# Other shares of 262 steps per batch among the stages of an audio tower kernel

## The reference, cut to what matters

```python
scores, idx = jax.lax.top_k(sim, 16)                       # 8 heads, two halves of a key, 64 keys each
score = scores[0][..., :, None] + scores[1][..., None, :]
final_scores, pk_idx = jax.lax.top_k(score, 16)            # 16 of the 256 sums
final_scores = softmax(final_scores)
k = einsum('bnhk,bnhkd->bnhd', final_scores, keys_table[ind])      # ind: 4096 rows per head
v = einsum('bnhk,bnhkd->bnhd', final_scores, values_table[ind])
attn = softmax(where(causal, q @ k, lowest));  out = attn @ v;  return out @ Wo
```

## Time and profile before

| what | value |
|---|---|
| three runs, median (lowest to highest) | 7954.98 us (7948.87 to 8025.97) |
| the profiled execution, its own time | 7943.69 us |
| its span, first to last instruction | 7941.9 us |
| mean granted TensorE clock | 0.941 of full |
| PE busy | 6697.2 us, 84% |
| ACT busy | 5005.2 us, 63% |
| POOL busy | 4498.3 us, 57% |
| DVE busy | 4120.9 us, 52% |

### The profile page before, as it was taken

The page is one execution under the profiler, slowest core; times in us unless marked ns, Lnnn a source line. Parts: engine busy times, 40 slices in busy tenths (PEclk is TensorE's granted clock), DMA queues, the critical chain, the costliest instruction groups (busy, mean ns, idle before and its releaser), DMA issues.

```text
span 7941.9 us, 139719 instructions
## 1 busy us (share of the span) xinstructions
PE 6697.2 (84%) x28800; PEld 3500.4 (44%) x28800; DVE 4120.9 (52%) x13711; ACT 5005.2 (63%) x10845; POOL 4498.3 (57%) x4108
## 2 busy tenths in 40 slices
PE   2789798897979889798888979889797988979977
PEld 1445354443535444353443535444353544435533
DVE  7472645627374472646537264562737447273146
ACT  0666576665757666576665657667575766667842
POOL 0575665656565565656556565565656556566610
PEclk9999899998999999899998989999898999999977
DMA  0111111111111111111111111111111111111100
GB/s 29 46 42 34 37 40 38 40 36 36 40 36 39 37 40 36 36 40 38 38 38 38 36 38 41 36 40 36 35 40 36 40 35 40 36 38 44 48 19 13
DMA packets 93887, 294.93 MB, mean 37 GB/s; under 512 B 17879, under 2 KB 26546, under 8 KB 92780
## 3 DMA queue, kind: packets, MB, share of 16 engines
q1 hardware_dynamic: 92748, 285.25, 11.2%
q10 hardware_dynamic: 288, 0.07, 0.0%
HBM read 280.68 MB, written 4.61 MB: 36 GB/s over the span
## 4 chain that ended last, share of the span: by engine, by line
PE 62%; DVE 27%; issue 6%; ACT 4%; DVEq 0%; ACTq 0%; POOL 0%; DMA 0%; SPq 0%; POOLq 0%
PE accu L505 24%; PE dense L491 7%; PE dense L512 7%; DVE picks L1231 6%; PE dense L493 6%; DVE picks L1225 4%; PE sims L623 2%; PE work L629 2%; PE sims L593 2%; DVE store L1235 2%; PE work L668 1%; DVE i L1173 1%; PE work L616 1%; PE work L551 1%; DVE picks L1205 1%
## 5 line engine op out<-in xcount | busy, mean ns | idle before, releaser
L440 POOL TENSOR_TENSOR dense_w<-dense_w,store 128x375 f32<-128x375 f32 x4096 | 4495.9, 1107 | 3092.4 <-ACT dense_w L878 3070.1
L505 PE MATMUL accu<-dense_w,store 128*128 128x375 f32 x8192 | 3365.4, 494 | 186.8 <-POOL dense_w L440 104.5
L883 ACT ACTIVATE past<-dense,edge 128x375 bf16<-128x375 f32 x4096 | 2351.8, 574 | 1195.5 <-PE dense L512 1172.5
L878 ACT ACTIVATE dense_w<-dense 128x375 f32<-128x375 f32 x4096 | 1955.5, 477 | 114.8 <-PE dense L493 107.0
L505 PEld LDWEIGHTS accu<-dense_w,store 128*128 128x128 f32 x8192 | 1430.1, 194 | 554.7 <-issue 334.9
L512 PE MATMUL dense<-store,hot 128*128 128x375 bf16 x4096 | 1338.0, 327 | 163.5 <-ACT past L883 159.4
L491 PE MATMUL dense<-store,spread 96*128 96x375 bf16 x4096 | 1353.1, 330 | 53.0 <-ACT dense_w L878 45.7
L493 PE MATMUL dense<-past,far 128*128 128x375 bf16 x4096 | 1356.8, 331 | 0.0
L512 PEld LDWEIGHTS dense<-store,hot 128*128 128x128 bf16 x4096 | 400.5, 98 | 1490.1 <-issue 1241.3
L491 PEld LDWEIGHTS dense<-store,spread 96*128 96x128 bf16 x4096 | 401.6, 98 | 839.4 <-issue 541.1
L1231 DVE TENSOR_TENSOR picks<-picks 125x2048 uint16<-125x2048 uint16 (+2 forms) x576 | 726.5, 1261 | 76.5
(11 more groups left out here) (248 smaller groups left out, 6497.6 us busy)
## 6 DMA issues: line engine op xcount, KB each, us to landing
store<-in SPq DMA_DIRECT2D x513, 512.0 KB, 3.5
x_in<-in SPq DMA_DIRECT2D x16, 187.5 KB, 2.4
store<-in SPq DMA_DIRECT2D x1, 2048.0 KB, 8.7
queries_kept<-n3T SPq DMA_DIRECT2D x16, 93.8 KB, 3.7
h_saved<-h SPq DMA_DIRECT2D x16, 93.8 KB
store<-queries_kept SPq DMA_DIRECT2D x16, 93.8 KB, 2.3
store<-h_saved SPq DMA_DIRECT2D x16, 93.8 KB
out<-store SPq DMA_DIRECT2D x16, 93.8 KB
```

Of the source, the lines that this page charges most:

```text
L440: nc.gpsimd.tensor_tensor(dense_w[:, i % RING, :], dense_w[:, i % RING, :], first_of[:, i // CHUNKS, :], ALU.mult).then_inc(s["weighed"], 1)
L505: last = mm(accu[:, 0, 0:S], table[:, n % PIECE_RING, i % PIECE, :], dense_w[:, i % RING, :], start=(c == 0), stop=(c == CHUNKS - 1))
L878: fn(dense_w[:, i % RING, :], dense[:, n % 2, 0:S], ACT.Relu).then_inc(s["taken"], 1)
L883: fn(past[:, j % 2, :], coded, ACT.Relu, bias=edge[:, 0:1]).then_inc(s["past"], 1)
```

## The change

Only the constants that share out the slots are changed. The sum stays 262 for each batch.

```diff
-FILL_PREPARE = (4, 3, 3, 4, 5, 4, 4, 4, 5)
-FILL_GRADIENT = (3, 6, 5, 6, 6, 6, 5)
+FILL_PREPARE = (2, 2, 2, 3, 4, 4, 4, 4, 4)
+FILL_GRADIENT = (2, 4, 4, 4, 4, 4, 4)
 PICKS_GRADIENT = (1, 1, 1, 1, 1, 1, 1)
-FILL_FIRST = (8, 18)
-FILL_SECOND = (24, 19)
+FILL_FIRST = (8, 36)
+FILL_SECOND = (34, 32)
 FILL_VO, FILL_QUERY, FIRST_HEAD = (2, 2, 2), 2, 4
-STEPS_A = (6, 6, 6, 6, 6, 6, 8, 8)
-STEPS_B = (6, 6, 6, 6, 6, 6, 6, 6)
+STEPS_A = (5, 5, 5, 5, 5, 5, 6, 5)
+STEPS_B = (5, 5, 5, 5, 5, 5, 4, 4)
 NEXT_FROM = 6
-FILL_LAST = (3, 5)
+FILL_LAST = (2, 4)
```

## The result

The changed kernel takes 7619.83 us, median of three runs (7617.11 to 7624.59), against 7954.98 before: a ratio of 0.9554, 95% interval 0.9471 to 0.9636. The forecast was 7630.

What follows compares the result with a forecast made beforehand. PE is busiest (84%), but DVE's picking ends both rounds, with PE waiting 27.6 us per batch. Removed 44.2 less added 21.7 us is 22.5 per batch, 325 us together: 7955 to 7630 us, range 7540 to 7790.

Steps and rivals of the forecast that it cites:

- The price of a step: Outside the rounds, each removed step gives back 1.18 us; 40 steps per batch are worth 47.2 us.
- Gradient: Of three steps (3.5 us) removed just ahead of L706, 2.4 us are lost; the stage's other steps count fully.
- Heads: Heads 0 to 5: PE moves up by 14.2 us, less 0.6 us for tight places; bounds 7.1 and 14.2.
- First round: Of 17 added steps 10 are free; 7 cost 8.3 us, less 2.9 us at the upper clock: 5.4 us.
- Second round: Of 23 added steps 8 fit the idle time; 15 cost 17.7 us, less 3.9 us at the upper clock: 13.8 us.
- POOL's 1.4 us: Added cost per batch in the rounds: POOL is held up a little longer beside DVE, 1.4 us.
- The 1.1 us for a copy of `accu`: Added cost per batch: one `accu` copy that PE waits out inside its long wait comes out of it.
- DVE binds the attention: Rival in the heads: DVE's picks of tile 2 leave PE only 7.1 us; 16 us per batch, 7725 us; chance 0.2.
- the slower rival: EARLY, preparation, heads: removed steps give back nothing, rounds still cost 21.7 us per batch; 8260 us; chance 0.04.
- POOL's pace for all steps: Rival in the rounds: POOL's 1.7 us holds for all added steps, 11.5 us gained per batch; 7788 us; chance 0.1.
- The full return: Rival in the rounds: all of PE's wait and slow stretches come back, 36.2 us per batch; 7436 us; chance 0.05.
- the fourth rival: Same as the slower rival: removed steps were cover, 8260 us, chance 0.04; sign: PE less busy in EARLY or heads.

Runs made afterwards that it cites:

- each round alone: Two kernels against the one before: only the first round gets more slots (26 to 44), 7798.65 us; only the second (43 to 66), 7748.87 us.
- the second round alone: Kernel before with more slots in the second round only (43 to 66), taken out of EARLY and the heads: 7748.87 us, ratio 0.9743.

## Why the prediction was right

- **What bounds the rounds.** L1261 ended them; with 18 and 23 steps more it doesn't, and the time goes. Shown by the waits (31 to 2) and by each round alone.
- **The price of a step, 1.18 us**, holds in EARLY and preparation to within 1.5 us per stage. It is a price at the upper clock, and the stages' clocks moved: EARLY from 0.97 to 1.00, the preparation from 0.99 to 0.94. The prediction has no term for the clock outside the rounds.
- **Gradient.** "I count 2.4 us, as much as that wait, as lost": the total was 0.9 us off (-9.7 for -10.6). The two slots taken at that place were the weak part of the change: with them back the gradient is 3.4 us shorter, most of it the clock. That I had not seen. Why the clock is lower there isn't settled by the length of the wait, as the two runs with one round alone show.
- **Heads.** 14.2 less 0.6 us expected, 16.9 measured, more than the upper bound. DVE's waits for the scores, 6.34, 3.34 and 4.11 us in the earlier trace rows, are now 0.36, 1.89 and 3.90 us, 7.6 us less where 7.1 were expected, and the end of picking is in time: L475 waits for L1261 nowhere in the loop. Of the further 3 us about 2 can be read from the stage's rows: the granted clock goes from 0.99 to 1.00 of 120 us (1.2 us, an estimate) and PE's idle time from 6.8 to 6.0 us. The last 1 us isn't settled.
- **First round.** +7.4 for +7.7 us, though "10 of the 17 are free" was low: with 37 slots in the round DVE was still last by 2.2 us. DVE ended 4.2 us later in the round than before (56.3 us after its start, not 52.1), and PE had 6.0 us more to do, not 8. So the sum came out nearer than its steps.
- **Second round.** 3.0 us too cheap: +18.2 for +15.2. The term that failed is "the similarities, the products L603 behind them (2.33 us, half of it saved) and a step come at the upper clock, 3.9 us". Only the similarities got faster, and nothing came of it, because L603 starts when PE's branch is through (5.72 us after the similarities began, against 3.97 before), and behind that idle time PE is at the lower clock again. PE had 10.5 us more to do than DVE there, not 18.
- **The small terms.** POOL's 1.4 us: PE's wait for it went from 7.8 to 9.0 us. The 1.1 us for a copy of `accu` that comes out of the long wait didn't show: those waits went from 4.6 us in five to 4.1 in four.
- **The sum.** 22.5 us per batch forecast, 23.8 measured; 325 and 335 us in all. The misses of the second round and of the heads have opposite signs and nearly cancel. The total is closer than its parts, and that is luck.
- **The rivals.** That DVE binds the attention is refuted by the second round alone and by the heads' 103.1 us. Cover that was lost (the slower rival) is seen in one place only, ahead of L706. POOL's pace for all steps is refuted by +7.4 us and by its own rows: 32 multiplications in 44.85 us and 35 in 49.83, 1.4 us each and not 1.7. The full return is refuted by the 9.0 us that PE still waits for POOL.
- **The signs.** The repeat time (447.1), the similarities at 1.95 us, L706's wait (4.3) and DVE's waits came as said. The rounds are 65.1 and 97.4 us long, not 63 and 93, and L593's wait in the whole span is 111.7 us, not a few tens. "PE less busy in EARLY" was to be a sign of the fourth rival and did come, 91% for 94%, though the stage lost 16.8 us: its idle time stayed at 3.7 and 3.9 us and the stage got shorter. The sign should have been idle time, not the share.

## What to carry to other kernels

Where work is dealt out by hand among stages, compare each engine's busy time with the stage's length, and move steps to the stage in which another engine ends last. Then look at the places from which they came one by one, at the waits and at the granted clock: where PE's wait had grown from 2.4 to 4.3 us, two steps put back were worth more than twice their own time. Don't take the work that lies beside an overhead for its cover until the overhead is taken away once: the hint on the kernel before showed that the loop's turn had cost its full price all along.

## What I had not expected of the hardware

- PE's branch at the end of a long loop took 3.3 to 5.4 us, those of the other engines about 0.05; with the prefetch hint 0.35 us. The same hint had no effect in one kernel that differs in the numbers of slots alone. Without the hint the branch takes 3.8 to 5.5 us in every kernel with 66 slots in the second round and 3.3 to 3.9 us in those with 43 or 53, whatever the first round has; why stays open.
- POOL and DVE held up each other, not only POOL: DVE's three minima took 4.33 us beside 375 columns of POOL's multiplication and 3.10 beside 75.
- Two groups of f32 matmuls with 64 rows each, one on the lower and one on the upper partitions, overlap in the records (L593 and L603), though the program has one behind the other.
- At one place of the program (L706) the matmuls ran at the lower clock behind a wait of 4.32 us and at the upper one behind 2.43 us; in two other kernels the same two matmuls took 0.97 us behind 4.47 us, the first of them at the upper clock, and 1.48 us, all at the lower, behind 2.48 us.
